# A two-layer graph network on one core: who places the bin groups, and six units instead of four between a tail sum's scaling and its addition

## The reference

```python
h = relu(layernorm(x))
for W_l, W_r, b in two layers:
    agg = segment_sum(h[src], dst) / max(count(dst), 1)
    h = relu(agg @ W_l + h @ W_r + b)
x = x + h
h = relu(layernorm(x))
m = relu(concat(h[src], h[dst]) @ W_interact + b_interact)
m = segment_sum(m, src) / 4
out = x + h + relu((h + m) @ W_update + b_update)
```

## Time and profile before

| | |
|---|---|
| median of three runs | 1517.28 us (1516.06 to 1519.37) |
| time of the profiled execution | 1513.23 us |
| its span, first to last instruction | 1511.4 us |
| PE busy | 1318.1 us (87%) |
| DVE busy | 1307.1 us (86%) |
| ACT busy | 939.7 us (62%) |
| POOL busy | 922.8 us (61%) |
| mean granted clock of TensorE | 0.950 |
| chain that ended last, by engine | DVE 38%, PE 35%, ACT 12%, issue 10% |

### The profile page before, as it was taken

The page is one execution under the profiler, slowest core; times in us unless marked ns, Lnnn a source line. Parts: engine busy times, 40 slices in busy tenths (PEclk is TensorE's granted clock), DMA queues, the critical chain, the costliest instruction groups (busy, mean ns, idle before and its releaser), DMA issues.

```text
span 1511.4 us, 40749 instructions
## 1 busy us (share of the span) xinstructions
PE 1318.1 (87%) x15612; PEld 1129.9 (75%) x15612; DVE 1307.1 (86%) x3899; ACT 939.7 (62%) x1831; POOL 922.8 (61%) x942
## 2 busy tenths in 40 slices
PE   1425989999999998999999679999999999999987
PEld 1213767777777766777777678898999999998987
DVE  7938899999999646677676779999999999999998
ACT  2645788878778730010000558888888888888886
POOL 5263408888781006777760167777777777777773
PEclk7755999999999999999999789999999999999999
DMA  3004536464646258999995134444444444444442
GB/s 124 0 1 137 212 133 252 159 254 154 259 158 231 76 158 280 299 308 301 297 297 183 43 96 123 123 130 131 129 133 127 122 142 123 131 124 129 129 121 65
DMA packets 121788, 241.71 MB, mean 160 GB/s; under 512 B 20184, under 2 KB 74601, under 8 KB 121594
## 3 DMA queue, kind: packets, MB, share of 16 engines
q1 hardware_dynamic: 95179, 187.74, 36.8%
q0 software_dynamic: 24832, 50.78, 13.3%
q10 hardware_dynamic: 1584, 0.59, 0.1%
HBM read 169.09 MB, written 73.14 MB: 160 GB/s over the span
## 4 chain that ended last, share of the span: by engine, by line
DVE 38%; PE 35%; ACT 12%; issue 10%; DMA 2%; SPq 1%; POOL 1%; ACTq 0%; DVEq 0%; POOLq 0%
PE ps L1271 13%; DVE room L2211 7%; ACT lnw L1132 6%; PE ps L1253 6%; DVE hot L1834 5%; PE ps L1242 4%; PE ps L1477 3%; DVE ps L2247 3%; DVE hot L2201 2%; DVE hot L1829 2%; DVE slab L2253 2%; PE ps L1311 2%; DVE keys L1960 2%; DVE keys L1959 2%; ACT slab L1153 1%
## 5 line engine op out<-in xcount | busy, mean ns | idle before, releaser
L1021 ACT ACTIVATE slab<-ps 128x980 f16<-128x980 f32 x256 | 321.5, 1277 | 93.0 <-PE ps L1242 85.5
L932 POOL DMA_INDIRECT cells<-b_rows,work x236 | 239.7, 1016 | 74.8 <-issue 68.9
L1477 PE MATMUL ps<-slab,room 125*128 125x128 f16 x3538 | 235.8, 220 | 34.2 <-DVE room L2211 31.7
L1253 PE MATMUL ps<-slab,room 128*128 128x320 f16 x1568 | 251.9, 300 | 0.1
L1132 ACT ACTIVATE lnw<-iota_w,keys 128x126 f32<-128x126 f32 x750 | 242.4, 389 | 0.0
L1477 PEld LDWEIGHTS ps<-slab,room 125*128 125x128 f16 x3538 | 206.5, 98 | 47.4 <-DVE room L2211 47.3
L1468 PE MATMUL ps<-inv,hot 125*128 125x128 f16 x1800 | 223.8, 220 | 4.9 <-DVE hot L2201 4.9
L1271 PE MATMUL ps<-slab,room 128*128 128x320 f16 x1568 | 227.0, 301 | 0.0
L896 POOL DMA_INDIRECT hot<-t_rows,pairs x160 | 166.0, 1038 | 54.8 <-issue 48.2
L1271 PEld LDWEIGHTS ps<-slab,room 128*128 128x128 f16 x1568 | 153.4, 98 | 59.5 <-issue 2.7
L1242 PE MATMUL ps<-hot 128*128 128x245 bf16 x1024 | 160.8, 282 | 36.5 <-DVE hot L1834 31.7
(11 more groups left out here) (373 smaller groups left out, 2392.4 us busy)
## 6 DMA issues: line engine op xcount, KB each, us to landing
slabs_d<-slab SPq DMA_DIRECT2D x14, 3920.0 KB, 13.3
slab<-slabs_d SPq DMA_DIRECT2D x98, 560.0 KB, 5.2
hot<-lane_d SPq DMA_DIRECT2D x50, 576.0 KB
inv<-inv_row SPq DMA_DIRECT2D x32, 160.0 KB, 7.6
keys<-up_d SPq DMA_DIRECT2D x25, 160.0 KB
room<-up_d SPq DMA_DIRECT2D x25, 160.0 KB
cells<-b_rows,work POOLq DMA_INDIRECT x236
t_rows<-room SPq DMA_DIRECT2D x1, 3200.0 KB, 12.8
```

The source lines that it names most:

```text
L932: p.indirect_dma_start(rows_g[gi % RS][:, j, :], None, b_rows, bass.IndirectOffsetOnAxis(ap=node_t[:, t:t + 1], axis=0)).then_inc(e_gath[g ...
L1021: a.activation(slab[par][:, :, u * UB * BW:(u + 1) * UB * BW].rearrange("p h (k d) -> p k h d", k=UB), psum_unit(u).rearrange("p k (h d) - ...
L1253: last = t.matmul(ps[:, 4 + s % 2, 0:SC], table[:, h, term, :], slab[s % 2][:, h, :], start=k == 0, stop=k == HI * HALVES - 1)
L1477: last = t.matmul(to, end_hot[g // 3][0:BN, u:u + P], bt[0:BN, bt_at(tile, w), k, :], start=False, stop=w == w1 - 1 and k == HALVES - 1)
```

## The change

The 52 placings are dealt out anew. POOL takes all 26 of the first half, seven behind each turn from turn 6 on (7, 7, 7 and 5), and 6 of the second half: 32 instead of 21. ACT takes 5 of the second half and none of the first: 5 instead of 22. DVE takes 15 of the second half instead of 9. And ADD_BEHIND goes from 4 to 6, in both layers. From line 844 on, the code of the kernel after stands one line higher or lower: the subtraction is line 845 and the placing's copy 841 on POOL, and VectorE's lines are one less (1798 for 1799, 1828 for 1829).

```diff
-        POOL_PLACES = [[k for k in range(HALF_W) if k % 2], [k for k in range(HALF_W, NW) if k % 3 == 1]]
-        ACT_PLACES = [[k for k in range(HALF_W) if k % 2 == 0], [k for k in range(HALF_W, NW) if k % 3 == 2]]
-        DVE_PLACES = [k for k in range(HALF_W, NW) if k % 3 == 0]
+        POOL_PLACES = [list(range(HALF_W)), [k for k in range(HALF_W, NW) if k % 5 == 1]]
+        ACT_PLACES = [k for k in range(HALF_W, NW) if k % 5 == 3]
+        DVE_PLACES = [k for k in range(HALF_W, NW) if k % 5 not in (1, 3)]
...
-        WEIGH_BEHIND, ADD_BEHIND = 2, 4
+        WEIGH_BEHIND, ADD_BEHIND = 2, 6
...
+        PER_TURN = 7
...
-                    for k in POOL_PLACES[0][4 * (c - PLACED_FROM):4 * (c - PLACED_FROM) + 4]:
+                    for k in POOL_PLACES[0][PER_TURN * (c - PLACED_FROM):PER_TURN * (c - PLACED_FROM + 1)]:
                         place(k)
...
-            for h in range(2):
-                act.wait_ge(k_half, h + 1)
-                for k in ACT_PLACES[h]:
-                    base = act.value_load(gbin_i[0:1, k:k + 1], min_val=0, max_val=KW)
-                    a.activation(cells_of[k % 2][:, bass.ds(base, KWIN)], k_win[:, k, :], ACT.Copy
-                                 ).then_inc(k_placed, 1)
+            act.wait_ge(k_half, 2)
+            for k in ACT_PLACES:
+                base = act.value_load(gbin_i[0:1, k:k + 1], min_val=0, max_val=KW)
+                a.activation(cells_of[k % 2][:, bass.ds(base, KWIN)], k_win[:, k, :], ACT.Copy).then_inc(k_placed, 1)
```

More of the change, by code:

```diff
@@ L316, in gnn_kernel @@
         HALF_W = NW // 2
-        POOL_PLACES = [[k for k in range(HALF_W) if k % 2], [k for k in range(HALF_W, NW) if k % 3 == 1]]
-        ACT_PLACES = [[k for k in range(HALF_W) if k % 2 == 0], [k for k in range(HALF_W, NW) if k % 3 == 2]]
-        DVE_PLACES = [k for k in range(HALF_W, NW) if k % 3 == 0]
-        assert sorted(sum(POOL_PLACES, []) + sum(ACT_PLACES, []) + DVE_PLACES) == list(range(NW))
+        POOL_PLACES = [list(range(HALF_W)), [k for k in range(HALF_W, NW) if k % 5 == 1]]
+        ACT_PLACES = [k for k in range(HALF_W, NW) if k % 5 == 3]
+        DVE_PLACES = [k for k in range(HALF_W, NW) if k % 5 not in (1, 3)]
+        assert sorted(sum(POOL_PLACES, []) + ACT_PLACES + DVE_PLACES) == list(range(NW))
         assert NT * D + KW + KWIN <= HI * SC // 2
@@ L849, in _ @@
                 if c >= PLACED_FROM:
-                    for k in POOL_PLACES[0][4 * (c - PLACED_FROM):4 * (c - PLACED_FROM) + 4]:
+                    for k in POOL_PLACES[0][PER_TURN * (c - PLACED_FROM):PER_TURN * (c - PLACED_FROM + 1)]:
                         place(k)
-            assert 4 * (NC - PLACED_FROM) >= len(POOL_PLACES[0])
+            assert PER_TURN * (NC - PLACED_FROM) >= len(POOL_PLACES[0])
             pool.wait_ge(k_half, 2)
```

## The result

The kernel after takes 1526.29 us (median of 20 runs, 1514.14 to 1532.81), the kernel before, run beside it, 1517.72. The medians differ by 8.6 us; the ratio of the executions is **1.005, 95% interval 1.0031 to 1.0069**, some 7.6 us slower, where I had forecast 5 us faster (range 1503.5 to 1516.5) and had given 0.04 to slower. The profiled execution of the kernel after took 1515.36 us, near the lower end of its runs, and its span is only 2.1 us longer than that of the trace before; so its trace shows how time is lost, but less of it than most executions lose.

What follows compares the result with a forecast made beforehand. VectorE was taken to set the pace in the first layer, TensorE in the second. Placings +0.5, first layer -5.5 and second layer 0 sum to -5.0 us: 1517.28 to 1512.3 us, range 1503.5 to 1516.5.

Steps and rivals of the forecast that it cites:

- Where the tables' addition starts: Prologue, line 1720: starts at 95.33, 9.7 us earlier, with POOL's last copy instead of ACT's the latest.
- The count beside the chain, predicted +0.5 us: Prologue: VectorE's count now lies beside POOL's chain of nine operations and ends at 115.6 against 115.13, losing the 9.7 gained.
- an operation with one input waits till the end of the running one of the chain: Prologue: VectorE's one-input operations take gaps between chain operations; the chain ends at 113.5, line 1775's five come behind it.
- one row: Prologue: addition 1720, begun at 105.03 inside a chain operation, took 1.52 and was not held, so two-input operations wait for nothing.
- the three rows of holding: Prologue: the CAST at 7.38, the subtraction at 46.59 and the chain's last operation, read as VectorE and POOL excluding each other.
- VectorE's waits for line 1317 go: First layer's tail additions: all 13 waits for TensorE's product, 7.3 us, vanish when the additions stand two units later.
- The first layer's gain, predicted -5.5 us: First layer: TensorE follows VectorE's 7.3 us, limited by the gathers' landing; bounds -7.7 and -4.3.
- the walk through the layer's lists: First layer, with the trace's durations: -7.6 for a landing of 1 us, -6.6 for 2, -5.6 for 3, -4.6 for 4.
- the range I had taken: First layer: landing of the gathers' data between 1 and 4 us, 3 us taken.
- The second layer, predicted 0: Second layer: VectorE's 20.5 us of waits are hidden by TensorE, which has no idle time, so nothing is gained.
- The rival on the slower side: First layer: VectorE's 7.3 us reappear at the one-hots' four slots, part 2 gives 0; say 1519.3 us, chance 0.08.

Runs made afterwards that it cites:

- e6_chain: Kernel after with the first layer's additions at 10 and POOL's chain held until the count's first rows are written, 1519.03 against 1514.1 us before, ratio 1.0027.
- e2_add6: Kernel before with ADD_BEHIND 6 instead of 4 alone, old placings: 1521.98 against 1514.38 us, ratio 1.0042.
- e3_half: Kernel after with every second gather of the first layer's tail left out: 1501.4 against 1514.38 us for the kernel before, ratio 0.9908.
- e7_memset: Kernel after with 24 idle one-column memsets by VectorE in the first layer: 1505.83 against 1514.1 us for the kernel before, ratio 0.9941.
- e9_l2add4: Kernel after with the idle first-layer memsets and the second layer's additions back at 4: 1504.54 against 1513.29 us for the kernel before, ratio 0.9936.
- e4_early: Kernel after with the first layer's tail groups started ten units earlier: 1521.56 against 1514.38 us for the kernel before, ratio 1.0041.

## Why the prediction was wrong, point by point

- **Where the tables' addition starts.** Right: 95.39 for 95.33, and POOL is the last to place. That it is right to 0.06 us is luck: POOL's last turn began at 87.94 instead of 87.15 and took 7.41 us instead of 7.85, and 0.3 had been added by guess.
- **The count beside the chain, predicted +0.5 us.** Right in that they collide, wrong in size: 5.05 us earlier at the end of line 1774, 4.20 at the first one-hot. The step that failed is that an operation with one input waits till the end of the running one of the chain. The five of line 1774 took 4.12 instead of 2.10 beside it; by that step they would have come behind the whole chain. And the two-input addition was held too, for 0.69 (2.21 for 1.52), which I had excluded by one row; line 1749, also with two inputs, was not (0.83 inside POOL's operation of 98.42 to 100.74, 0.82 with POOL idle in e6_chain). Of the three rows of holding the CAST's was weak too: it began ahead of the IOTA (7.38 and 7.41), so it was the earlier one that got longer. e6_chain puts the whole of the collision at 4.7 us; I had put it at 10.2. So this half of the change gave more than forecast, and the loss lies in the other half.
- **VectorE's waits for line 1317 go.** Right: they are gone in the first layer.
- **The first layer's gain, predicted -5.5 us.** Wrong, and this is what turned the sign: +1.6 in the trace, and e2_add6 is 0.42% slower in all. The step that failed is the walk through the layer's lists, which took the gathers' durations as given and only their landing as unknown. The landing was in the range I had taken (1.6 to 3.8 us where TensorE waited). The durations were not given: they depend on VectorE's pauses, which the change removes. The 140 gathers took 239.4 and 241.3 us instead of 231.6. The gain that I had worked out for gathers that don't bind (-7.6 to -7.7) is what e3_half and e7_memset show (-8.5 and -8.4).
- **The second layer, predicted 0.** Wrong: +3.8 in the trace, +6.7 in e2_add6, by the same step. TensorE "has no idle time" there, but its tail groups wait for gathers too, and these take 224.0 us instead of 220.5 (225.7 in e2_add6), with one of 3.14 us where none had been over 1.5. VectorE's waits, which cost nothing by themselves, had let them through; e9_l2add4 brings the waits back, and with them 221.1 us.
- **The rival on the slower side** named the place where VectorE would stand (line 1828, the four slots; it stands there 10.9 us) but not the reason: TensorE had idle time enough.

What stays open. The runs of the kernel after spread over 19 us; that the holds fall differently from one execution to the next would explain it, but each kernel has one trace, so this is argued, not shown. The edges' 2.3 us were not followed. And what in VectorE's stream holds a gather, and why only some gathers are caught, isn't settled: a stop of VectorE, an operation with an operand in PSUM, a memset and even a one-column addition end a hold; of the two tiny operations only the memsets made the sum smaller.

## What to carry to other kernels

A wait of an engine can be a resource of another one: before a wait is removed, look at what ends inside it on the engines that share a path with the waiting one, above all GpSimd's gathers beside a VectorE that hardly pauses (busy 96 to 97% of the stretch 240 to 440 us here). Look at the longest instances of an instruction and at what ends them, not only at its mean: ten of 140 gathers held the sign of this change. And where such a neighbour must get through, a tiny operation that does nothing can be worth more than the wait it replaces (24 memsets of 0.06 us: from a ratio of 1.005 to one of 0.994), but it has to be tried: as many one-column additions at the same places gave nothing (1.0052).

## What the runs showed of the hardware that I had not expected

- A gather issued by GpSimd takes 0.94 to 1.5 us as a rule, or is held, for up to 7.8 us in all (8.1 in e4_early), while VectorE runs operations with both operands in SBUF back to back. A held one ends 0.8 to 0.9 us behind VectorE's next stop or the start of its next operation with an operand in PSUM. The Trainium skill, SBUF — State Buffer, section "Who interferes with whom", says that a DMA which seems stalled by VectorE was one whose descriptors GpSimd could not write; the traces agree in that the time is spent in GpSimd's own instruction. The same section of the Trainium skill reports that tensor_tensor did not do this and infers why; here stretches of nothing but tensor_tensor with both operands in SBUF did (254.06 to 260.92 us in the kernel after, in a gather of 7.76 us).
- Beside each other, VectorE's and GpSimd's ordinary operations hold each other for a part of their time only: a count of 10.0 us took 4.7 us more beside a chain that is 17.4 us long and took 18.8.
- A stop of TensorE can cost more than itself. Right behind its waits of 2.22 and 4.69 us the granted clock is 0.50 (1.2 GHz instead of 2.4), from 271.0 to 274.4 and from 335.9 to 342.7 us, and the sums behind them took 1.58 and 1.86 us where the others take 1.06; behind another wait of 2.23 us (before 391.41) it stayed at 1.00.
